# Perceiver block on one core: another free slot in the weight plan, a transposed output evicted in halves, and the first weights loaded by the scalar engine's queue in four chunks

## What is computed

```python
def _L0_xattn_ref(x, latents, mask, g_x, b_x, g_l, b_l, w_q, w_kv, w_out, g_o, b_o):
    xn, ln = _ln(x, g_x, b_x), _ln(latents, g_l, b_l)
    q = ln @ w_q
    k, v = jnp.split(jnp.concatenate([xn, ln], axis=1) @ w_kv, 2, axis=-1)
    ...                                  # 8 heads, scaled scores, mask, softmax, weighted sum
    return _ln(out @ w_out, g_o, b_o)

x = x + _L0_xattn_ref(ctx_1024, _layernorm(x), mask, ...)
x = x + _L0_attn_ref(_layernorm(x), ...) # self attention of the 64 latents: rotary q and k,
                                         # o = o1 - lam * o2, RMS norm * ln_w + ln_b, @ Wo.T
x = x + _L0_ffn_ref(_layernorm(x), ...)  # fp4 quantised gate, up and down, width 1408
```

## Time and profile before

| | us |
|---|---|
| median of 3 runs | 1013.35 (1012.75 to 1017.39) |
| the profiled execution, its own time | 1013.17 |
| its span, first to last instruction | 1011.20 |
| outside the span | 1.97 |
| PE busy | 973.2 |
| DVE busy | 792.4 |
| ACT busy | 441.0 |

### The profile page before, as it was taken

The page is one execution under the profiler, slowest core; times in us unless marked ns, Lnnn a source line. Parts: engine busy times, 40 slices in busy tenths (PEclk is TensorE's granted clock), DMA queues, the critical chain, the costliest instruction groups (busy, mean ns, idle before and its releaser), DMA issues.

```text
span 1011.2 us, 16850 instructions
## 1 busy us (share of the span) xinstructions
PE 973.2 (96%) x6564; PEld 795.8 (79%) x6564; DVE 792.4 (78%) x1692; ACT 441.0 (44%) x823; POOL 146.1 (14%) x163
## 2 busy tenths in 40 slices
PE   5999999999999999999999999999999999999997
PEld 4887888878788788788788788886767678888885
DVE  7455688798797897996986985477888688899985
ACT  4534565365365465456456446443333332222221
POOL 1320011211211211210210210012313100000000
PEclk9999999999999999999999999999999999999999
DMA  7856233443352442442441445042000740000000
GB/s 252 246 165 211 69 99 89 121 124 85 100 141 69 112 131 66 114 128 65 125 129 44 124 118 169 8 149 93 1 2 2 276 182 11 11 11 11 11 11 21
DMA packets 72447, 98.52 MB, mean 97 GB/s; under 512 B 38320, under 2 KB 47152, under 8 KB 70064
## 3 DMA queue, kind: packets, MB, share of 16 engines
q1 hardware_dynamic: 65008, 72.80, 24.5%
q0 software_dynamic: 7360, 24.65, 7.6%
HBM read 67.54 MB, written 29.88 MB: 96 GB/s over the span
## 4 chain that ended last, share of the span: by engine, by line
PE 72%; DVE 18%; ACT 5%; issue 3%; DMA 1%; POOL 0%; SPq 0%; DVEq 0%; ACTq 0%
PE ps_banks L146 17%; PE ps_banks L148 17%; PE ps_banks L147 17%; PE ps_banks L433 8%; PE ps_banks L552 3%; PE ps_banks L529 2%; PE ps_banks L677 2%; PE ps_banks L678 2%; PE ps_banks L679 2%; DVE sb_b_stats L777 1%; DVE sb_wq_big L943 1%; DVE sb_w_q L951 1%; DVE sb_ctx L790 1%; DVE sb_kT_lo L816 1%; ACT sb_zT_hi L1365 1%
## 5 line engine op out<-in xcount | busy, mean ns | idle before, releaser
L146 PE MATMUL ps_banks<-sb_zT_hi,sb_wkv_hi 128*128 128x512 f32 x256 | 105.9, 414 | 0.0
L146 PE MATMUL ps_banks<-sb_wkv_hi,sb_zT_hi 128*128 128x512 f32 x256 | 104.8, 410 | 0.0
L148 PE MATMUL ps_banks<-sb_wkv_hi,sb_zT_lo 128*128 128x512 f32 x256 | 100.4, 392 | 0.0
L148 PE MATMUL ps_banks<-sb_zT_hi,sb_wkv_lo 128*128 128x512 f32 x256 | 100.2, 392 | 0.0
L147 PE MATMUL ps_banks<-sb_zT_lo,sb_wkv_hi 128*128 128x512 f32 x256 | 100.0, 390 | 0.0
L147 PE MATMUL ps_banks<-sb_wkv_lo,sb_zT_hi 128*128 128x512 f32 x256 | 99.8, 390 | 0.0
L1321 ACT ACTIVATE sb_kT_hi<-ps_banks 128x512 fp32r<-128x512 f32 x64 | 38.1, 596 | 138.6 <-PE ps_banks L148 138.6
L146 PE MATMUL ps_banks<-sb_wgu,sb_z_hi 128*128 128x512 f32 (+1 forms) x192 | 73.7, 384 | 0.0
L147 PE MATMUL ps_banks<-sb_wgu,sb_z_hi 128*128 128x512 f32 (+1 forms) x192 | 72.1, 376 | 0.0
L148 PE MATMUL ps_banks<-sb_wgu,sb_z_lo 128*128 128x512 f32 (+1 forms) x192 | 72.0, 375 | 0.0
L816 DVE TENSOR_TENSOR sb_zT_lo<-sb_zfull,sb_zT_hi 128x512 fp32r<-128x512 f32 x64 | 44.2, 691 | 31.4 <-ACT sb_zT_hi L1365 31.4
(11 more groups left out here) (247 smaller groups left out, 2480.7 us busy)
## 6 DMA issues: line engine op xcount, KB each, us to landing
sb_ctx<-in_ctx SPq DMA_DIRECT2D x16, 1024.0 KB, 5.9
sb_wgu<-scratch_wgu SPq DMA_DIRECT2D x8, 1024.0 KB, 9.9
scratch_wgu<-sb_w_hi POOLq DMA_DIRECT2D x22, 256.0 KB, 3.6
scratch_wgu<-sb_w_lo POOLq DMA_DIRECT2D x22, 256.0 KB, 3.8
sb_wdn<-scratch_wdn SPq DMA_DIRECT2D x2, 2816.0 KB, 9.5
scratch_q<-sb_a_qk POOLq DMA_DIRECT2D x8, 512.0 KB, 6.2
sb_qpack<-scratch_q SPq DMA_DIRECT2D x32, 128.0 KB, 5.9
sb_wgu<-scratch_wgu SPq DMA_DIRECT2D x4, 768.0 KB, 10.1
```

The source lines that it names most:

```text
L146: e.matmul(o, wh, xh, start=i == 0, stop=False)
L148: m = e.matmul(o, wl, xh, start=False, stop=i == n - 1)
```

## The change

Three places are edited. In `weight_plan` the free slot moves from slot 3 of the even batches to slot 1 of the odd ones. `copy_out` evicts the bank in two halves of 256 columns, each with a semaphore of its own, and `project_o` starts its first two chunks after the first half. `w_q` is loaded by ACT in four chunks of 256 KB, issued ahead of ACT's first activation; ACT and DVE split it chunk by chunk, in turn with the chunks of the latents, and PE's first transposes go row tile by row tile into four banks at once.

```diff
     for b in range(1, NB):
         for slot in range(8):
-            if slot != 3 or b % 2:
+            if slot != 1 or b % 2 == 0:
                 advance((b, slot), 4)
...
+            def turn_first_latents():
+                on.wait_ge(consts_landed, 32)
+                banks = [claim(("lnT", 0, c), ring_a) for c in range(C)]
+                for k in range(4):
+                    on.wait_ge(x_normed, k + 1)
+                    for c, bank in enumerate(banks):
+                        m = e.transpose(psum[:, bank, k * P:(k + 1) * P], x_in[:, k, c * P:(c + 1) * P], ident[:, :])
+                        if k == 3:
+                            m.then_inc(filled[bank])
+
             def first_queries():
-                on.wait_ge(w_lo_split, 1)
                 banks = [claim(("q", 0, n), ring_a) for n in range(C)]
                 for c in range(C):
+                    on.wait_ge(wq_lo_split, c + 1)
                     on.wait_ge(ln_lo_done, c + 1)
...
             def project_o(t):
-                bank, nth = took["oT", t]
-                on.wait_ge(drained[bank], nth)
                 on.wait_ge(d_w_landed[3], 16)
                 bank = claim(("o_out", t))
-                plain(psum[:, bank, :], t_t[t % 2], w_d[3]).then_inc(filled[bank])
+                for c in range(C):
+                    if c == 0:
+                        on.wait_ge(t_half_done, t + 1)
+                    if c == C // 2:
+                        from_bank, nth = took["oT", t]
+                        on.wait_ge(drained[from_bank], nth)
+                    m = e.matmul(psum[:, bank, :], t_t[t % 2][:, c, :], w_d[3][:, c, :], start=c == 0, stop=c == C - 1)
+                m.then_inc(filled[bank])
...
-            for c in range(C):
-                turn_latents(0, c)
+            turn_first_latents()
             first_queries()
...
-            split_lo(w_raw[:, :, :], wq_hi[:, :, :], wq_lo[:, :, :], w_hi_split, 1, w_lo_split)
-            lo_of_latents(0, 0)
-            nth = latent_stats(1, 0, 4)
-            for c in range(1, C):
+            for c in range(C):
+                split_lo(w_raw[:, c, :], wq_hi[:, c, :], wq_lo[:, c, :], wq_hi_split, c + 1, wq_lo_split)
                 lo_of_latents(0, c)
+                if c == 1:
+                    nth = latent_stats(1, 0, 4)
...
-                e.activation(t_t[t % 2][:, :, :].rearrange("p c n -> p (c n)"), psum[:, bank, :], ACT.Identity,
-                             bias=lnwb[:, 1:2], scale=lnwb[:, 0:1]).then_inc(drained[bank])
+                for half, done in enumerate((t_half_done, drained[bank])):
+                    e.activation(t_t[t % 2][:, 2 * half:2 * half + 2, :].rearrange("p c n -> p (c n)"),
+                                 psum[:, bank, half * D // 2:(half + 1) * D // 2], ACT.Identity,
+                                 bias=lnwb[:, 1:2], scale=lnwb[:, 0:1]).then_inc(done)
...
-            on.wait_ge(wq_landed, 16)
-            copy(wq_hi[:, :, :], w_raw[:, :, :], w_hi_split)
+            w_q_rows = a["w_q"].rearrange("(c p) n -> p c n", p=P)
             for c in range(C):
+                copy_bits(e, w_raw[:, c, :], w_q_rows[:, c, :]).then_inc(wq_landed[c], 16)
+            for c in range(C):
+                if c == 0:
+                    on.wait_ge(wq_landed[0], 16)
+                    copy(wq_hi[:, 0, :], w_raw[:, 0, :], wq_hi_split)
                 hi_of_latents(0, c)
+                if c + 1 < C:
+                    on.wait_ge(wq_landed[c + 1], 16)
+                    copy(wq_hi[:, c + 1, :], w_raw[:, c + 1, :], wq_hi_split)
...
-            copy_bits(e, w_raw[:, :, :], rows("w_q")).then_inc(wq_landed, 16)
             copy_bits(e, x_in[:, 4:8, :], rows("x")[:, 4:8, :]).then_inc(x_landed[4], 16)
...
-            on.wait_ge(w_lo_split, 1)
+            on.wait_ge(wq_lo_split, C)
             copy_bits(e, w_raw[:, :, :], rows("w_out")).then_inc(w_out_landed, 16)
```

More of the change, by code:

```diff
@@ L353, in perceiver @@
         x_landed = sems("x_landed", 5)
-        wq_landed, wk_landed, wv_landed, w_out_landed = (sem(f"w{n}_landed") for n in ("q", "k", "v", "_out"))
+        wq_landed = sems("wq_landed", C)
+        wk_landed, wv_landed, w_out_landed = (sem(f"w{n}_landed") for n in ("k", "v", "_out"))
         pow_set = sem("pow_set")
@@ L359, in perceiver @@
         w_hi_split, w_lo_split = sem("w_hi_split"), sem("w_lo_split")
+        wq_hi_split, wq_lo_split = sem("wq_hi_split"), sem("wq_lo_split")
         q_hi_done, kl_hi_done = sem("q_hi_done"), sem("kl_hi_done")
@@ L382, in perceiver @@
         d_scored, d_maxed, d_exped, a_ready = sem("d_scored"), sem("d_maxed"), sem("d_exped"), sem("a_ready")
-        o_sq_summed, o_scaled = sem("o_sq_summed"), sem("o_scaled")
+        o_sq_summed, o_scaled, t_half_done = sem("o_sq_summed"), sem("o_scaled"), sem("t_half_done")
         wgu_landed, wdn_landed = sems("wgu_landed", NP), sem("wdn_landed")
@@ L463, in latent_key @@
                 on.wait_ge(ln_lo_done, C * (half + 1))
-                on.wait_ge(w_lo_split, 2)
+                on.wait_ge(w_lo_split, 1)
                 bank = claim(("kl", half, n), ring_a)
@@ L471, in latent_value @@
                 on.wait_ge(ln_lo_done, C * (half + 1))
-                on.wait_ge(w_lo_split, 3)
+                on.wait_ge(w_lo_split, 2)
                 bank = claim(("vl", half, k), ring if half else ring_a)
@@ L539, in project_out @@
                 on.wait_ge(tile_lo_done, t + 1)
-                on.wait_ge(w_lo_split, 4)
+                on.wait_ge(w_lo_split, 3)
                 bank = claim(("y", t))
@@ L548, in turn_y @@
                 transposes(bank, [y[t % 2][:, c * P:(c + 1) * P] for c in range(C)]).then_inc(filled[bank])
-            def plain(o, w, x):
-                for c in range(C):
-                    m = e.matmul(o, w[:, c, :], x[:, c, :], start=c == 0, stop=c == C - 1)
-                return m
             def project(t, which):
@@ L1183, in vector_program @@
                 lo_of_latents(1, n)
-            split_lo(w_raw[:, :, :], w_out_hi[:, :, :], w_out_lo[:, :, :], w_hi_split, 4, w_lo_split)
+            split_lo(w_raw[:, :, :], w_out_hi[:, :, :], w_out_lo[:, :, :], w_hi_split, 3, w_lo_split)
             on.wait_ge(ln_lo_done, 2 * C)
```

4 lines of the change are left out of this document (2 added, 2 removed).

## The result

The changed kernel takes 1004.9 us (median of 4, 1003.12 to 1005.17) against 1013.92 for the kernel before beside it: a ratio of 0.9895 on record, 95% interval 0.9879 to 0.9911; the quotient of these two medians is 0.9911, the upper end of it. In the later comparisons, with up to 23 executions of the kernel before, that one's median was 1015.07 to 1015.25. The 1013.35 on which the forecast rests was the median of its first three. The time forecast was met; the terms of the sum were not, as the rows show.

A forecast was written before the change was run, and what follows sets the result against it. PE, busy for 973.2 of 1011.2 us, was taken to bound the kernel. Gains of 5.4 (slot), 2.2 (halves) and 0.8 us (start) sum to 8.4 off 1013.17: 1004.8, or 1004.9 as median; range 1002.8 to 1008.2.

The forecast's parts named there:

- Part 1: Weight plan: moving the free slot removes PE's waits for the quantised weight tile, 5.4 us, kept 4.4 to 5.6.
- the six waits go as a whole: Odd batches: all six PE waits for sb_w_q vanish, taken as 5.4 us.
- The margins of 1.1 and 1.5 us: Odd batches: context rows ready 1.1 us before PE needs them, the weight tile 1.5 us before.
- The even batch: Slots 0 to 3: 2.08 us of DVE idle time cover 1.6 more; 0.72 us take up the rest, nothing paid.
- Part 2: Output eviction: a half takes 0.50 us instead of 0.78, eight sb_tT waits shorten by 0.28 each, 2.2 us.
- Rival (b): Output eviction: halves bring nothing, ACT starting late or paying the whole fixed cost again; 1007.2 us; chance 0.08.
- Part 3: Kernel start: loading and splitting w_q by chunks brings the keys' first product earlier, 0.8 us, kept -1.4 to 1.7.
- F = 12.1: Kernel start: F, when the first transposed bank is full, comes at 12.1 us, with rows 2.1 us late; gain 0.8.
- F + 2.1 and F + 14.1: Kernel start: the first product and the keys' first product come 2.1 and 14.1 us after the first transposed bank fills.
- rival (a): Kernel start: rows of x come much later, making the start 1.3 us slower than before; 1007.1 us; chance 0.16.
- (c): Weight plan: the tile wait moves to slot 4 of odd or slot 2 of even batches; 1010.3 us; chance 0.10.
- (d): Even batches: 1.6 us of quantiser work not hidden in each of seven, PE waiting for sb_probs; 1016.2 us; chance 0.04.

The follow-up runs named there:

- free_odd_3: The changed kernel with the free slot in slot 3 of the odd batches instead of slot 1; 1014.14 us, ratio 0.9994.
- start_only: The kernel before with the new start and nothing else; 1014.25 us, ratio 0.9993.
- q_by_sync: The changed kernel with the w_q chunks issued on the sync engine's queue behind the rows of x and the constants; 1000.48 us, ratio 0.9853.
- slot_and_halves: The changed kernel with the start of the kernel before; 1004.28 us, ratio 0.9894.
- before_again: The kernel before once more, unchanged, for a second profile of its start; 1012.96 us.
- slot_only: The kernel before with the new weight plan and nothing else; 1007.14 us, ratio 0.9919.

## Why the prediction was right, and where it was not

**The time** was right because errors cancelled. Profile against profile the sum said 8.4 off; from the keys on it was 11.2, and the start took 1.3 back: 9.9. The base was 1.7 us too low: 8.4 off the 1015.1 of many executions is 1006.7. The sum was too small by about what the base was too low.

**Part 1** was right in mechanism and place and mis-sized: 10.3 where the sum had 5.4 and kept 5.6 at most. The step that failed is "the six waits go as a whole", by which the recorded waits were taken as the price. The prediction also said that PE shows no wait for the two context rows behind the stall. It shows none, and yet had one: the rows ended at 278.65 and PE took them at 278.71, which stood in the earlier trace rows and one row of PE further. With it the stall was 1.24 instead of 1.02 us, and the drained pipe, the slower transposes and the hidden wait for `sb_v` make it 1.80 for each pair of batches. The margins of 1.1 and 1.5 us came out at 0.3 and 1.3. The even batch was right: idle time gone, 0.72 us untouched. "The free slot stands where DVE has time, and not where it is late" is what free_odd_3 bears out.

**Part 2**: 1.2 us instead of 2.2, under the kept 1.8. A half costs 0.56 us, the value from the constant difference of the earlier trace rows. The step that failed is the choice of 0.50 by the ratio, "because the ratio fits an engine that pays by the column for the most part". And PE starts 0.15 us after the first half's end (708.66), 0.05 after the whole one's in the earlier trace rows, which nothing in the prediction had: 0.78 + 0.05 - 0.56 - 0.15 = 0.12 for each of eight waits, 1.0 of the 1.2 us. Why PE starts later behind a half isn't shown. Rival (b) was half true. The estimate of 0.51 from the Trainium skill, ScalarE: Activation LUTs, Rules for kernel authors, was 0.05 us too low for the half (0.56) and for the whole (0.78): the measurement decides. It counts the bias; this eviction also reads a scale for each row, and no run here shows whether that is the difference.

**Part 3**: profile against profile 1.3 us slower instead of 0.8 faster, of which 0.6 is the slow products; by the time of start_only 0.7 faster, between 1.6 and -0.3. The rows of `x` 2.1 us late was right (2.18). The step that failed is F = 12.1: it delayed only the last row, with one transpose behind it. But DVE normalises all four rows back to back behind the last statistics, so PE's first transpose comes at 10.51, and thirteen of them at 0.21 us fill the bank near 13.4, where the sum had 12.1. From there F + 2.1 and F + 14.1 held within 0.4 us, less the slow products. The prediction's reading of these transposes, "at a granted clock of 1.00 (2.4 GHz)", was wrong as well: their spacing is that of the lower level, at the upper one it is 0.11 us. It did no harm to the sum, since the old start's transposes ran at the same level. That the rows come late is rival (a)'s mechanism, and its 1.3 us slower is what the profile shows, by F = 13.4 and the slow products instead of its F = 14.2. The Trainium skill's rule in DMA: Bandwidth & Descriptors, Issuing engines are not separate DMA queues, is borne out in that the two loads interleave on the same engines: 4.9 us for the rows against 3.2 in q_by_sync. That a second queue is no gain in bandwidth isn't: 386 against 341 GB/s from 3 to 6 us, 374 against 310 from 6 to 9. The prediction's "more is in flight" was right, and it didn't save the rows. The deeper error was to price the old start from one execution.

Rivals (c) and (d) didn't come: PE shows no wait for `sb_w_q` or `sb_probs` anywhere.

## What to carry over

Price a stall by when the pipeline catches up, not by its row: measure the same stretch (here two batches, or the scores before a transpose) with and without the stall, and look at the next producer on the late engine, since removing the first wait helps only when the second comes early too. Put slack ahead of the place where the producer is late: behind it, in slot 3, it was worth nothing here, though the tile's own deadline had moved just as far. What depends on DMA landings needs more than one profile, and a second queue for data that isn't needed first delayed what is. Where the profile's clock and the spacing of equal matmuls disagree, see whether the trace has a record of the clock there at all.

## What was not expected of the hardware

- One and the same load of 1 MB, issued at the same place, took 6.0, 6.3, 7.8, 7.9 and 8.0 us in five profiles. Which of these a kernel gets wasn't settled.
- In 9 of 14 profiles 3 to 11 of PE's first products took 0.63 us or so instead of 0.39 and stood 0.43 us apart instead of 0.23. All of these ran at the lower clock: in five the clock had risen and fallen again, in four no rise is recorded between PE's first transpose and them, and the transposes had the slow spacing too (slot_and_halves: first transpose at 9.69, rise at 21.28 us). The profile's 1.00 in those four stands for a stretch without a record.
- before and before_again have the same code and start PE at 9.93 and 9.71 us; the clock's rise is recorded at 13.95 us in one and at 17.67 in the other.
- In slot_only the granted clock was 0.95 from 14 us to the end, 0.50 for a few us early on, and stages B and D each took 1.2 to 1.3 us longer than in the kernels with the same code there.
- An ACT eviction with scale and bias costs 0.46, 0.56, 0.67 and 0.78 us for 128, 256, 384 and 512 columns.
